# Graph attention on one core: node numbers as 16-bit words, and three per-pass updates moved to Pool

## What is computed

```
w     = silu(edge_attr_32 @ rad_W1 + b) @ rad_W2 + b + silu(edge_attr_32_n2 @ sph_W1 + b) @ sph_W2 + b   # per edge, 128 wide
q     = (x @ Wq)[dst]                 # row of the edge's target
k, v  = (x @ Wk)[src], (x @ Wv)[src]  # rows of the edge's source
alpha = sum over 16 of (q * w * k) / 4 * edge_weight          # one number for each of 8 heads
out   = segment_sum(alpha * v, dst) / 16
y     = layernorm(x + out)
```

## Time and profile before

| | us |
|---|---|
| median of 3 runs | 1994.96 |
| lowest and highest of them | 1991.69 and 1996.93 |
| the profiled execution | 1993.38 |
| its span, first to last instruction | 1992.0 |
| first and last gather of L615 issued | 40.6 and 1973.7 |
| busy POOL / PE / DVE | 1492.8 / 1726.2 / 1626.7 |

### The profile page before, as it was taken

One profiled execution on the slowest core, in us unless ns is written; L12 is line 12 of the kernel. 1 busy time (PEld: TensorE's weight loads), 2 busy tenths in 40 slices (PEclk: granted clock), 3 DMA queues, 4 the chain that ended last, 5 costly groups with the idle time before them and its releaser, 6 DMA issues. The chain is left out here.

```text
span 1992.0 us, 56803 instructions
## 1 busy us (share of the span) xinstructions
PE 1726.2 (87%) x14497; PEld 1256.5 (63%) x14497; DVE 1626.7 (82%) x4334; ACT 576.0 (29%) x1019; POOL 1492.8 (75%) x1565
## 2 busy tenths in 40 slices
PE   8799999999898898888898888888888888888887
PEld 7566666666666566666666655666666656666665
DVE  5589988989888878888887878888888878888787
ACT  5332323222222222222222322222222222222222
POOL 6777777777777777777777777777777777777775
PEclk9799999999999989998999999999989989999888
DMA  9755555555555555555555555555555555555553
GB/s 327 253 158 159 161 159 152 156 160 160 155 152 162 160 156 151 161 156 150 161 144 161 147 159 155 149 158 147 159 145 159 155 149 149 156 157 149 158 146 94
DMA packets 197258, 319.01 MB, mean 160 GB/s; under 512 B 82965, under 2 KB 110342, under 8 KB 196934
## 3 DMA queue, kind: packets, MB, share of 16 engines
q0 software_dynamic: 74304, 202.47, 35.5%
q1 hardware_dynamic: 113564, 105.88, 18.4%
q10 hardware_dynamic: 9066, 7.03, 1.5%
HBM read 300.46 MB, written 14.74 MB: 158 GB/s over the span
## 5 line engine op out<-in xcount | busy, mean ns | idle before, releaser
L615 POOL DMA_INDIRECT kvt<-kvtab,srcS x1532 | 1466.5, 957 | 473.4 <-issue 465.8
L713 ACT ACTIVATE hs<-bank,B 128x512 f32<-128x512 f32 x806 | 510.5, 684 | 1370.8 <-issue 766.0
L653 PE MATMUL bank<-W2r,hs 128*128 128x128 f32 x3224 | 499.2, 302 | 10.6 <-ACT hs L713 10.3
L653 PEld LDWEIGHTS bank<-W2r,hs 128*128 128x128 f32 x3224 | 423.5, 205 | 89.4 <-issue 71.3
L877 DVE TENSOR_TENSOR t<-bank,kvt 128x512 f32<-128x512 f32 (+1 forms) x397 | 266.2, 671 | 251.5 <-DMA kvt<-kvtab,srcS 136.9
L653 PE MATMUL bank<-W2s,hs 128*128 128x128 f32 x3224 | 455.0, 287 | 0.0
L653 PEld LDWEIGHTS bank<-W2s,hs 128*128 128x128 f32 x3224 | 423.6, 205 | 0.0
L668 PE MATMUL bank<-msg,oh 128*32 128x128 f32 x3224 | 179.8, 294 | 225.2 <-DVE accT L808 222.4
L668 PEld LDWEIGHTS bank<-msg,oh 128*32 128x32 f32 x3224 | 72.1, 110 | 416.5 <-issue 379.6
L894 DVE TENSOR_REDUCE bank<-t 128x32 f32<-128x512 f32 x403 | 280.1, 695 | 13.9
L630 PE MATMUL bank<-eft,W 32*128 32x512 f32 x1612 | 275.9, 672 | 2.9 <-ACT kvh L448 2.4
(11 more groups left out here) (100 smaller groups left out, 674.7 us busy)
## 6 DMA issues: line engine op xcount, KB each, us to landing
kvA<-kvtab ACTq DMA_DIRECT2D x3968, 1.0 KB
eft<-in_ef SPq DMA_DIRECT2D x102, 512.0 KB, 7.3
kvS<-kvtab SPq DMA_DIRECT2D x3200, 1.0 KB
kvt<-kvtab,srcS POOLq DMA_INDIRECT x1532
dbt<-dst SPq DMA_DIRECT2D x102, 192.0 KB, 6.3
qwt<-qtab SPq DMA_DIRECT2D x403, 24.0 KB
kvtab<-kvt SPq DMA_DIRECT2D x24, 256.0 KB, 7.4
qtab<-qx SPq DMA_DIRECT2D x12, 384.0 KB, 6.0
```

Source lines behind the costliest of these rows:

```text
L615: pool.indirect_dma_start(kvt[:, (g - HX) % KS, t, :], None, kvtab, bass.IndirectOffsetOnAxis(ap=srcS[:, g * TG + t:g * TG + t + 1], axis= ...
L653: pe.matmul(WB[g % 2][:, t * D:(t + 1) * D], hs[:, g % HS, j, t * 128:(t + 1) * 128], w2[:, :], start=(j == 0 and t == 0), stop=False, ski ...
L713: act.activation(hs[:, g % HS, j, :], HB[i % 4][:, :], ACT.Silu, bias=B1[:, j:j + 1]).then_inc(m_si, 1)
```

## The change

Three things change.

1. **Bytes become 16-bit words.** `dst8` (uint8) becomes `dst16` (int16), and so does `dbt`, which doubles to 12 KB a partition. `window_T` now reads int16 and still writes bf16; the comparison is with the whole node number, so `basep` is made directly from `base` (`nodep` and its low byte go). Each broadcast of L368 moves twice the bytes. In the first stage the copy at L469 reads whole int32 numbers (now from a part of `dbt` itself and not from `cutS`) and writes int16; for that reason ACT no longer waits for `s_db` before it loads the rest of `cutS`.
2. **The updates for a further pass move from DVE to POOL**, after POOL's last gather and ahead of its wait for the landings. They are five instructions instead of six.
3. **The last windows.** `window(401)` now stands in its regular place behind L894 of group 401, and `window(402)` ahead of group 402.

```diff
-        dbt = sb("dbt", [128, DS, 4, G], u8)
+        dbt = sb("dbt", [128, DS, 4, G], i16)
...
-            low_bytes = dbt[:, :, :, :].rearrange("p b a g -> p (b a g)")[:, 0:T]
+            dst_words = dbt[:, :, :, :].rearrange("p b a g -> p (b a g)")
-            dbi = cutS[:, :].bitcast(i32)
+            db16 = dst_words[:, 0:T]
+            dbi = dst_words[:, T:3 * T].bitcast(i32)
...
-            link(dve.tensor_scalar(nodep[:, :], base[0:WP, :], pidx, None, ALU.add))
-            dve.tensor_copy(basep[:, :], low_byte(nodep)).then_inc(s_win, 1)
+            dve.tensor_scalar(basep[:, :], base[0:WP, :], pidx, None, ALU.add).then_inc(s_win, 1)
...
-                             dst8[4 * b:4 * b + 4, :].rearrange("(o a) g -> o (a g)", o=1)
+                             dst16[4 * b:4 * b + 4, :].rearrange("(o a) g -> o (a g)", o=1)
...
-                    dve.tensor_copy(low_bytes, low_byte(dbi)).then_inc(s_db, 1)
+                    dve.tensor_copy(db16[:, :], dbi[:, :]).then_inc(s_db, 1)
...
-                    sp.dma_start(flat(dst8), low_bytes).then_inc(s_do, 16)
+                    sp.dma_start(flat(dst16), db16[:, :]).then_inc(s_do, 16)
...
-            act.wait_ge(s_db, 1)
             act.dma_start(cutS[:, SE:T], cutT[:, SE:T]).then_inc(s_cut2, 16)
...
-                if g == NE - 2:
-                    window(NE - 2)
+                if g == NE - 1:
                     window(NE - 1)
-                    next_rel()
-                    next_base()
-                if g == NE - 1:
                     accumulate(NE - 4)
                     collect(NE - 3)
-                    if (NE - 1) % 4:
-                        next_baseq()
...
-                if g < NE - 2:
+                if g < NE - 1:
                     window(g)
...
-            if (NE - 1) % 4:
-                next_basei()
             accumulate(NE - 1)
...
+            last_start = 4 * ((NE - 1) // 4)
+            pool.wait_ge(m_ot, NE)
+            pool.tensor_scalar(base[:, :], base[:, :], float(W), None, ALU.add).then_inc(m_up, 1)
+            pool.tensor_scalar(basep[:, :], basep[:, :], float(W), None, ALU.add).then_inc(m_up, 1)
+            pool.wait_ge(m_oh, NE)
+            pool.tensor_scalar(rel[:, :], rel[:, :], -float(W), None, ALU.add).then_inc(m_up, 1)
+            pool.wait_ge(m_up, 1)
+            pool.wait_ge(m_q, last_start + 1)
+            pool.wait_ge(m_acc, last_start + 1)
+            pool.tensor_copy(basei[:, :], base[0:1, :]).then_inc(m_up, 1)
+            pool.tensor_scalar(baseq[:, :], base[0:1, :], float(QROW), None, ALU.mult).then_inc(m_up, 1)
+            pool.wait_ge(m_up, 5)
             for i in range(KS):
                 pool.wait_ge(m_kv[i], 16 * sum(gathered(g) for g in range(HX + i, NE, KS)))
```

More of the change, by code:

```diff
@@ L60, in gnn_program @@
     i32 = mybir.dt.int32
-    u8 = mybir.dt.uint8
+    i16 = mybir.dt.int16
     ALU = mybir.AluOpType
@@ L98, in gnn_program @@
     qtab = nc.dram_tensor("qtab", [NQ, NPART * D], bf16, kind="Internal").ap()
-    dst8 = nc.dram_tensor("dst8", [NG, G], u8, kind="Internal").ap()
+    dst16 = nc.dram_tensor("dst16", [NG, G], i16, kind="Internal").ap()
+    u8 = mybir.dt.uint8
     KVROW, QROW = 4 * 2 * D, 2 * NPART * D
@@ L126, in gnn_program @@
         basep = sb("basep", [WP, NG], f32)
-        nodep = sb("nodep", [WP, NG], i32)
         basei = sb("basei", [1, NG], i32)
@@ L185, in psb @@
                 return pre.enter_context(nc.sbuf_tensor(name, shape, dt))
-            assert T <= ES * 2 * G and T <= DS * 4 * G
-            low_bytes = dbt[:, :, :, :].rearrange("p b a g -> p (b a g)")[:, 0:T]
+            assert T <= ES * 2 * G and 3 * T <= DS * 4 * G
+            dst_words = dbt[:, :, :, :].rearrange("p b a g -> p (b a g)")
             dsti = eft[:, :, :, :].rearrange("p k a g -> p (k a g)")[:, 0:T].bitcast(i32)
-            dbi = cutS[:, :].bitcast(i32)
+            db16 = dst_words[:, 0:T]
+            dbi = dst_words[:, T:3 * T].bitcast(i32)
             d0i = psb("d0i", [128, NG], i32)
@@ L303, in grouped @@
                 return t.rearrange("p (g t) -> p g t", t=TG)
-            def low_byte(t):
-                return t[:, :].bitcast(u8).rearrange("p (g b) -> p g b", b=4)[:, :, 0]
             def spread(t):
@@ L809, in accumulate @@
                                   ALU.add).then_inc(m_acc, 1)
-            def next_rel():
-                dve.wait_ge(m_oh, NE)
-                dve.tensor_scalar(rel[:, :], rel[:, :], -float(W), None, ALU.add).then_inc(m_up, 1)
-            def next_base():
-                dve.wait_ge(m_ot, NE)
-                dve.tensor_scalar(base[:, :], base[:, :], float(W), None, ALU.add).then_inc(m_up, 1)
-                dve.tensor_scalar(nodep[:, :], nodep[:, :], float(W), None, ALU.add).then_inc(m_up, 1)
-                dve.wait_ge(m_up, 3)
-                dve.tensor_copy(basep[:, :], low_byte(nodep)).then_inc(m_up, 1)
-            def next_baseq():
-                dve.wait_ge(m_q, 4 * ((NE - 1) // 4) + 1)
-                dve.wait_ge(m_up, 4)
-                dve.tensor_scalar(baseq[:, :], base[0:1, :], float(QROW), None, ALU.mult).then_inc(m_up, 1)
-            def next_basei():
-                dve.wait_ge(m_q, NE)
-                dve.wait_ge(m_up, 4)
-                dve.tensor_copy(basei[:, :], base[0:1, :]).then_inc(m_up, 1)
             def tiles(t):
```

4 lines of the change are left out of this document (removed).

## The result

| | before | after |
|---|---|---|
| median of 5 runs, us | 1991.69 | 1982.52 |
| lowest and highest | 1988.90 and 1996.93 | 1980.05 and 1984.69 |
| profiled execution, its span | 1993.38, 1992.0 | 1980.05, 1978.8 |

The ratio of the times is 0.9949, 95% interval 0.9932 to 0.9967: the changed kernel is faster by 6.6 to 13.5 us, 10.2 at the middle (9.2 by the two medians). 1985 had been forecast from a median of 1995.0, or 10.1 less. The two profiled executions are 13.3 us apart, since that of after is the lowest of its five; what follows explains this pair. All medians and ratios in this document leave out one execution, one of nine of `e6_twice_words`, which took 5167 us.

A forecast was written before the change was run, and what follows sets the result against it. The prediction took POOL's unbroken chain of gathers as the bound. The chain's -11.5 us and the end's +1.4 made -10.1, giving 1985 us from a median of 1995.0, range 1979 to 1992.

The forecast's parts named there:

- The bound: POOL issues gathers without a pause, 1.25 us a step; DVE or PE savings count only if they shorten a gather.
- The length of `window_T`: DVE's comparison on int16 would take 0.346 us instead of 0.477, the middle between no change and 0.214.
- The holds: Main-loop gathers lengthened by DVE's `window_T` and `window`: 16.1 us in sum, to fall by 11.5.
- `window` behind held-up `window_T`s: 42 gathers held up because `window` follows a delayed `window_T` by about one gather step; gain 3.2 us.
- the point at 0.13: 0.13 us after its start, a gather needs something that `window_T` or `window` holds for its whole length.
- The end: Stretch behind the last gather's start: POOL finishes after DVE, costing 1.4 us more, between -1.0 and +9.8.
- I take 7.3: Reload of POOL's code behind its last gather, 7.3 us, taken from a 512 KB transfer in the main loop.
- the first rival: POOL's reload is nearly free, DVE decides the end, which gives 1.0 us: 1982.5 us; chance 0.12.
- I take 4.0: POOL's five update instructions behind the last gather take 4.0 us, between 3.1 and 7.0, priced from its fills.
- the wait for the last window: POOL's wait for DVE's last window, at about 4 us behind the last gather's start, lies inside the reload.
- The start: First stage up to and around the first gathers: no change, within 0.5 us either way.
- DVE's wait for rows: DVE's first product would still wait over 130 us for gathered rows to land; 136.9 us in the kernel before.

The follow-up runs named there:

- e6_twice_words: The changed kernel with `window_T` issued twice per group, the first into a table nobody reads: 1985.43 us, ratio 0.9964 to the kernel before.
- n_halves: The kernel before, bytes kept, with each `window_T` cut into two instructions of 256 elements: 3110.69 us against 3093.69, ratio 1.0044.
- w_halves: The kernel before, bytes kept, with each `window_T` cut into two instructions of 256 elements: 3139.24 us against 3122.43, ratio 1.0068.
- e3_noupd: The changed kernel without POOL's updates for a further pass: 3085.01 us against 3100.06 for the kernel before, ratio 0.9944.
- n_rel_act: The changed kernel with the update of `rel` on ACT instead of POOL: 3083.86 us against 3100.49 for the kernel before, ratio 0.9938.
- n_words: The changed kernel with the updates back on DVE and both last windows ahead of group 401: 3079.62 us against 3100.18 before, ratio 0.9939.

## Why the prediction was right, point by point

**The bound.** Right. POOL's wait for DVE stayed at 8.2 us, the step at 0.946 + 0.30, and `e6_twice_words` shows that DVE's load can rise by 51 us above that of before while the time falls. The view of waits told this before the change, and the busy line did not the earlier trace rows.

**The length of `window_T`.** 0.346 forecast, 0.344 measured, but as the middle of two ends 0.26 apart: the rows of before could not have told it from any other value between, so by them alone it is luck. This was the step with the largest risk. The Trainium skill (VectorE: DVE Perf Modes, "The perf-mode tier table") gives a `tensor_scalar` on 2-byte data in SBUF half the time per element that it takes on 4-byte data. The trace agrees, with bytes in the place of the 4-byte data: behind the fixed 0.214, 0.130 us for 512 elements, where bytes took 0.263.

**The holds.** Right in the sum (4.6 and 4.6 us) and in each part, within 6 cases and 0.2 us. The 3.2 us of `window` behind held-up `window_T`s went for the reason given: none of the 74 in after holds a gather, where 42 of 90 did. `n_halves` and `w_halves` show that a shorter instruction is enough for short holds, with bytes too, and `e6_twice_words` that each instruction counts by itself. The longest early hold by `window_T` is the instruction's length less 0.21 to 0.24 us in every kernel: 0.477 and 0.256 in before, 0.344 and 0.116 to 0.133 in the nine kernels with 0.344. The Trainium skill (SBUF — State Buffer, "Who interferes with whom") says that an instruction in a mode with two ports keeps the pair that it shares with GpSimd for its whole length and the other is blocked; the traces agree, as each early hold ends with its `window_T`. The same section says that an instruction with two SBUF inputs contends with a GpSimd instruction that reads SBUF, but infers that it does not disturb the making of descriptors; here `window`, which has two, holds 64 gathers for 5.2 us. DVE's four long instructions that read at most one tile of SBUF (L877, L892, L894, L912) do not: in before they lie over the point at 0.13 in some 770 gathers, whose median excess is 0 to 1 ns. Two readings of before in the forecast were a little off, and nothing hung on them: of the 91 `window_T` over 0.50 us, 80 end 1.19 into a gather and 11 end 0.46 into one, and the later point lies at 0.83, not 0.79.

**The end.** The forecast's +1.4 came out as -0.2, and two terms were mis-sized in opposite directions. "I take 7.3" for the reload: 0.11 us lie between the last gather's end and POOL's first arithmetic, and no cost of the reload is visible, as in the premise of the first rival. "I take 4.0" for the arithmetic: it takes 8.5 us (1.25 + 1.22 + 4.28 + 0.51 + 1.22), more than the forecast's upper end of 7.0. The rows of fills, 0.8 ns an element, were the wrong kin: with an input to read and to add to, it is (4.28 - 1.25) / 1212 = 2.5 ns. A third term was counted as hidden and was not: the wait for the last window, 1.33 us, lay inside the forecast's reload and now stands by itself. So POOL ended at S + 10.8 and not at S + 12.9, S the last gather's start. DVE ended at S + 10.27, forecast 10.5. With no reload and arithmetic of 4.0, as the first rival had it, DVE would have decided, and by `e3_noupd` 0.9 us more been gained. That rival's time, 1982.5, is the median of after, but by chance: it was reckoned down from 1995.0, and before's own median is now 1991.7.

The Trainium skill's rule (GPSIMD Engine Reference, "Instruction dispatch") of about 6 us for a first call into freshly loaded code does not show in this trace: the gap is 0.11 us, and among the five behind it the only idle time is the 1.33 us that wait for DVE. Whether the instruction loaded anything here, or when, no run shows.

**The start.** The forecast had zero for the first stage "within 0.5 us either way". The first gather starts 1.0 us earlier, and the first stage's gathers were then held up for 1.05 us more, so nothing is left in the sum but each is twice the bound. Why the first gather is earlier was not settled; it was 39.7 in `e6_twice_words` as well.

**The sum.** Between the two profiled executions 10.1 us were forecast and 13.3 came. The 3.2 are the end (1.6), the start (1.0) and small things in the chain (0.5). That the ratio's middle gives 10.2 us, 0.1 from the forecast, is luck: its interval reaches from 6.6 to 13.5, and the forecast's sum had the end wrong by 1.6.

**What was to be seen.** Of the signs named, these came: L757 at 0.344 and 0.573 at the longest (forecast 0.35 and 0.60), gathers' busy time 1454.9 (1449 + 5), last gather at 1960.7 (near 1962; 13.0 us earlier, where 11 to 12 were named), DVE's end. Two did not: the gap of 7 us on POOL, and DVE's wait for rows, which fell to 105.7 where over 130 was named. That sign was badly chosen. DVE's product waits for whichever of rows and PE's bank comes last, and the waits for the bank rose from 119.6 to 146.5 us; only their sum hardly moved. That a lower number there does not bear on the bound is seen from POOL's own wait.

**What stays open.** Which part of the 10.2 us belongs to the words and which to the moves was not measured on a chip where the gathers are the bound. By the traces the words have the 11.5 us of the main loop, since the moves alone leave the holds as they were, and the moves have the end: DVE is done 1.2 us earlier behind the last gather's start (S + 10.3, where it was S + 11.5), and 0.9 of that is given back through POOL.

## What to carry to other kernels

When an engine that issues gathers without a pause is the bound, look for the few long ones among them and lay them beside what the vector engine does at their start: here it is the length of the single instruction there that lengthens the chain, so a faster form of it (here a 2-byte type) can pay even where that engine has time to spare. The same work in pieces gives the same short holds, but its price in time was not measured where gathers are the bound. Work moved to the engine that ends last is not free because it stands behind its last task; price it by an instruction of the same kind and not by a fill. When a change has several parts, ask of each part whether its own signature is in the trace, since two terms that are wrong in opposite directions can give the right sum.

## What was not expected of the hardware

- POOL's `tensor_scalar` on float32 takes 2.5 ns an element of a partition: 1.25 us for 404, 4.28 us for 1616. DVE does the same 1616 in 1.00 us, ACT in 1.55. A cast of one partition's 404 elements took POOL 0.51 us.
- PE restarts 1.46 us behind POOL where POOL comes last at the barrier, in all four kernels of that kind, and 1.03 to 1.06 behind DVE where DVE does, but 1.37 in `n_rel_act`.
- The same kernel takes 1992 us on one chip and 3094 to 3122 us on others. There PE, DVE, ACT and POOL are all idle together in 82 to 97 stretches of over 1.5 us, 163 to 190 us in sum (none in before's trace), TensorE's granted clock is 0.77, and DVE's product shows over 800 us of waits that end in an event from outside the core's own engines (`remote` in the rows of `n_words`). The cause is open. On those chips the words gave 15 to 21 us, the halves cost 17, and `window` in another place, with the same instructions on DVE, gave 13 to 15, so a time taken there says nothing on the gathers.
